# The Wf product of a two-layer graph network and routed FFN kernel, taken in rounded and rest parts in place of fp32

## The reference, cut to what matters

```python
def gnn(x, adj, W1, b1, W3, b3, Wf, bf):     # x: 2048 x 256, adj: 2048 x 2048, weights: 256 x 256
    h = relu(adj @ (x @ W1) + b1)
    h = relu(adj @ (h @ W3) + b3)
    return tanh(h @ Wf + bf)

x = x + gnn(layernorm(x), adj, ...)
x = x + routed_ffn(layernorm(x))             # 8 experts, top 2, hidden 1024, out = (silu(x@W1[e]) * (x@W3[e])) @ W2[e]
```

## Time and profile before

| | |
|---|---|
| median of 3 runs | 667.63 us (667.21 to 668.91) |
| profiled execution, its own time | 671.28 us |
| its span | 669.2 us |
| TensorE busy | 612.0 us (91%) |
| VectorE busy | 341.6 us (51%) |
| ScalarE busy | 312.5 us (47%) |
| GpSimd busy | 147.5 us (22%) |

### The profile page before, as it was taken

One profiled execution on the slowest core, in us unless ns is written; L12 is line 12 of the kernel. 1 busy time (PEld: TensorE's weight loads), 2 busy tenths in 40 slices (PEclk: granted clock), 3 DMA queues, 4 the chain that ended last, 5 costly groups with the idle time before them and its releaser, 6 DMA issues.

```text
span 669.2 us, 11466 instructions
## 1 busy us (share of the span) xinstructions
PE 612.0 (91%) x3472; PEld 519.8 (78%) x3473; DVE 341.6 (51%) x752; ACT 312.5 (47%) x589; POOL 147.5 (22%) x143
## 2 busy tenths in 40 slices
PE   1999999999999988989888999999999999999970
PEld 1888888887867676768767898888888888888860
DVE  3786434465646676636644333337333636377620
ACT  1567565766455465446522223335333536356520
POOL 3000000000000505027444123322332233223222
PEclk9999999999999999999989999999999999999985
DMA  8995000020002673521163022117111715376312
GB/s 303 359 333 203 5 1 1 0 95 1 1 3 92 123 177 119 159 64 41 17 194 90 10 33 34 29 21 219 32 28 19 219 32 147 88 211 166 80 29 32
DMA packets 34739, 63.74 MB, mean 95 GB/s; under 512 B 4954, under 2 KB 27100, under 8 KB 32636
## 3 DMA queue, kind: packets, MB, share of 16 engines
q1 hardware_dynamic: 26044, 52.32, 23.9%
q0 software_dynamic: 8224, 10.53, 9.7%
q10 hardware_dynamic: 432, 0.39, 0.2%
HBM read 54.02 MB, written 10.26 MB: 96 GB/s over the span
## 4 chain that ended last, share of the span: by engine, by line
PE 81%; DVE 4%; issue 4%; ACT 4%; DMA 3%; POOL 1%; SPq 0%; POOLq 0%; ACTq 0%; DVEq 0%
PE bank L1551 40%; PE bank L1420 8%; PE bank L1422 8%; PE bank L1421 8%; PE bank L1396 4%; PE bank L1598 4%; PE bank L1447 3%; DMA adj_s<-in_adj 2%; PE bank L1433 2%; PE bank L1384 2%; PE bank L1544 1%; DVE ring L915 1%; PE bank L1471 1%; POOL slot_rows L479 1%; PE bank L1445 1%
## 5 line engine op out<-in xcount | busy, mean ns | idle before, releaser
L1551 PE MATMUL bank<-ew,xeT 128*128 128x512 f32 x840 | 202.2, 395 | 4.6 <-DVE ew L1246 2.6
L1551 PEld LDWEIGHTS bank<-ew,xeT 128*128 128x128 f32 x840 | 154.7, 188 | 36.3 <-issue 4.2
L915 DVE TENSOR_TENSOR ring<-adj_s,ring 128x512 fp32r<-128x512 f32 x128 | 87.6, 689 | 76.5 <-ACT adj_s L596 40.8
L1551 PE MATMUL bank<-ew,heT 128*128 128x256 f32 x840 | 112.0, 291 | 4.7 <-issue 2.4
L1420 PE MATMUL bank<-ring,Z 128*128 128x512 f32 x256 | 110.1, 430 | 6.3 <-DVE ring L915 4.7
L1551 PEld LDWEIGHTS bank<-ew,heT 128*128 128x128 f32 x840 | 105.5, 196 | 6.2 <-issue 6.1
L1422 PE MATMUL bank<-ring,Z 128*128 128x512 f32 x256 | 100.6, 393 | 0.0
L1421 PE MATMUL bank<-ring,Z 128*128 128x512 f32 x256 | 100.2, 391 | 0.0
L512 POOL DMA_INDIRECT out<-y_st,idx_st x29 | 45.5, 1569 | 191.0 <-ACT y_st L748 169.0
L479 POOL DMA_INDIRECT slot_rows<-val,route x32 | 35.9, 1122 | 224.1 <-issue 222.4
L754 ACT ACTIVATE sil<-bank 128x512 f32<-128x512 f32 x58 | 34.6, 596 | 86.3 <-PE bank L1551 86.3
(11 more groups left out here) (183 smaller groups left out, 620.4 us busy)
## 6 DMA issues: line engine op xcount, KB each, us to landing
w_raw<-in_L_ffn_W SPq DMA_DIRECT2D x24, 1024.0 KB
adj_s<-in_adj SPq DMA_DIRECT2D x16, 1024.0 KB, 6.7
x_in<-in_x SPq DMA_DIRECT2D x4, 512.0 KB, 5.3
x_res<-in_x SPq DMA_DIRECT2D x4, 512.0 KB, 3.6
out<-x SPq DMA_DIRECT2D x4, 512.0 KB, 3.9
ffn_in_rows<-x_res SPq DMA_DIRECT2D x4, 512.0 KB
xg<-ffn_in_rows,idx POOLq DMA_INDIRECT x39
Wg<-in_L_gnn_W SPq DMA_DIRECT2D x2, 256.0 KB, 3.8
```

The lines of the kernel that those rows point to most:

```text
L915: nc.vector.tensor_tensor(lo, src, hi, ALU.subtract).then_inc(s_lo, 1)
L1551: last = nc.tensor.matmul(out_ap, stat[:, sl, k, :], w_at(k, wl), start=(k == k0 and sl == wl == 0), stop=(k == k1 - 1 and sl == 1))
```

## The change

The Wf product is taken like the others, from hi and lo parts. `hidden2` now handles one half `f` of the features at a time and writes two results, the rounded `hTs[:, 0]` and the whole `hTf[:, 1]`, with one activation each; its two halves stand at steps 1 and 2 of the next band in place of both at step 1. `h2_lo` on VectorE takes the rest at step 3. Wf itself is split once into `Wfs`, on VectorE, at step 8 of band 0. Each tile of `wf_rows` has six fp32r matmuls in place of two fp32 ones. `wf_rows` stands at steps 4 and 5 (before 2 and 3), and what comes after it moves too: `tanh` to 5 and 6 (3 and 4), `residual` to 6 and 7 (4 to 6), `spread` to 7 (6), the roots to 8 and 9 (7 and 8), `normal` to 9 and 10 (8 and 9), `xn_T` and `gate` one step later each. `top2`, `chosen`, `places`, `expert_order` and the expert's weights keep their steps. `hTs` is there once, while `hT` was there for two bands in turn: `hidden2` waits for the tiles of the band before. The last four gathered tiles go to `xge_b`, in the space of `Z`, so their gathers wait for the last step; the wait for `s_up` ahead of all of them is gone. Of `first_up(0, 0)` only the second half waits for `hidden2` of the last band, and that only for its first half.

```diff
@@ -73,12 +73,12 @@
         bf_hi = at("bf_hi", [2, D], F32R, 178)
-        hT = at("hT", [P, 2, KD, CW], F32, 176)
         hTs = at("hTs", [P, 2, KD, CW], F32R, 176)
...
         W3s = at("W3s", [P, 2, KD, D], F32R, 196)
+        Wfs = at("Wfs", [P, 2, KD, D], F32R, 198)
         route = at("route", [P, KB // 2], F32, 196)
@@ -93,7 +93,8 @@
         xeT0 = at("xeT0", [P, 2, KD, P], F32R, 172)
-        xge = at("xge", [P, EARLY, D], F32, 174)
+        xge_a = at("xge_a", [P, 2, D], F32, 174)
+        xge_b = at("xge_b", [P, EARLY - 2, D], F32, 156)
@@ -228,6 +229,8 @@
         s_w3s = sem("s_W3_split")
+        s_wfs = sem("s_Wf_split")
+        s_h2lo = sem("s_hT_layer2_lo")
         s_z2p = sem("s_z2_psum")
@@ -327,6 +330,10 @@
+        def first_rows(t):
+
+            return xge_a[:, t, :] if t < 2 else xge_b[:, t - 2, :]
+
         def first_xe_p(t):
@@ -483,7 +490,7 @@
                 nc.gpsimd.indirect_dma_start(
-                    out=xge[:, t, :], out_offset=None, in_=table[:, :],
+                    out=first_rows(t), out_offset=None, in_=table[:, :],
                     in_offset=bass.IndirectOffsetOnAxis(ap=first_idx[:, t:t + 1], axis=0),
@@ -529,9 +536,10 @@
             pool.wait_ge(s_xn1st, 32)
-            pool.wait_ge(s_up, CT * (NC - 1))
             for t in range(1, EARLY):
                 pool.wait_ge(s_xge, 16 * t)
+                if t == 2:
+                    pool.wait_ge(s_mm, 2 * S1)
                 first_gather(t)
@@ -610,16 +618,15 @@
-            def hidden2(c):
+            def hidden2(c, f):
                 act.wait_ge(s_mm, S1 + NT * (c + 1))
-                if c >= 2:
-                    act.wait_ge(s_up, CT * (c - 1))
+                if c >= 1:
+                    act.wait_ge(s_up, CT * c)
                 else:
                     act.wait_ge(s_z2p, NT)
-                for f in range(KD):
-                    last = nc.scalar.activation(hT[:, c % 2, f, :], acc[c % 2][f][:, :], ACT.Relu,
-                                                bias=bT[:, 1, f:f + 1])
+                for out_f in (hTs[:, 0, f, :], hTf[:, 1, f, :]):
+                    last = nc.scalar.activation(out_f, acc[c % 2][f][:, :], ACT.Relu, bias=bT[:, 1, f:f + 1])
                 last.then_inc(s_h2, 1)
@@ -650,12 +657,12 @@
-                if k in (3, 4):
-                    tanh(c, k - 3)
-                if k == 7:
+                if k in (5, 6):
+                    tanh(c, k - 5)
+                if k == 8:
                     roots(NC + c + 1)
-                if k in (10, 11):
-                    xn_T(c, k - 10)
+                if k in (11, 12):
+                    xn_T(c, k - 11)
                 if k == NT:
@@ -697,8 +704,8 @@
                     hidden1(s // NT - 1, jb - 1)
-                if jb == 1 and s > S1 + NT:
-                    hidden2(c - 1)
+                if jb in (1, 2) and s > S1 + NT:
+                    hidden2(c - 1, jb - 1)
                 if layer == 0 and c == NC - 1 and 2 <= jb < NT - CT + 2:
@@ -779,7 +786,8 @@
-            hidden2(NC - 1)
+            for f in range(KD):
+                hidden2(NC - 1, f)
             gap_exp(2)
@@ -924,6 +932,12 @@
                                         ALU.subtract).then_inc(s_hlo, 1)
+
+            def h2_lo(c):
+
+                dve.wait_ge(s_h2, KD * (c + 1))
+                nc.vector.tensor_tensor(hTs[:, 1, :, :], hTf[:, 1, :, :], hTs[:, 0, :, :].bitcast(F32),
+                                        ALU.subtract).then_inc(s_h2lo, 1)
@@ -1082,15 +1096,14 @@
-                tiles = {4: (0, 1), 5: (2,), 6: (3,)}.get(k, ())
-                residual(c, tiles)
-                if k == 6:
+                residual(c, {6: (0, 1), 7: (2, 3)}.get(k, ()))
+                if k == 7:
                     marked()
                     spread()
-                if k == 8:
+                if k == 9:
                     roots(NC + c + 1)
-                if k in (8, 9):
-                    normal(c, (2 * k - 16, 2 * k - 15))
+                if k in (9, 10):
+                    normal(c, (2 * k - 18, 2 * k - 17))
                 if k == NT - 2:
@@ -1169,6 +1182,13 @@
                     z_lo(NT - CT + jb - 7)
+                if layer == 1 and c == 0 and jb == 8:
+                    dve.wait_ge(s_z2p, NT)
+                    settle(nc.vector.tensor_copy(Wfs[:, 0, :, :], Wg[:, 2, :, :]))
+                    nc.vector.tensor_tensor(Wfs[:, 1, :, :], Wg[:, 2, :, :], Wfs[:, 0, :, :].bitcast(F32),
+                                            ALU.subtract).then_inc(s_wfs, 1)
+                if layer == 1 and c >= 1 and jb == 3:
+                    h2_lo(c - 1)
                 if layer == 1 and c >= 2:
@@ -1280,6 +1300,7 @@
             nc.vector.tensor_copy(first_idx[:, 1:EARLY], first_info[:, 1:EARLY, 0]).then_inc(s_fidx, 1)
+            h2_lo(NC - 1)
             residual(3, (0, 1))
@@ -1409,7 +1430,7 @@
                     else:
-                        pe.wait_ge(s_h2, n - 1 - NC)
+                        pe.wait_ge(s_h2, KD * (n - 1 - NC))
                     if n >= NC + 2:
@@ -1438,14 +1459,16 @@
                 for i in (2 * pair, 2 * pair + 1):
-                    pe.wait_ge(s_h2, c + 1)
+                    pe.wait_ge(s_h2lo, c + 1)
                     if c == 0:
+                        pe.wait_ge(s_wfs, 1)
                         pe.wait_ge(s_z2, NT)
...
                     for f in range(KD):
-                        last = nc.tensor.matmul(token_out(c, i), hT[:, c % 2, f, i * P:(i + 1) * P], Wg[:, 2, f, :],
-                                                start=False, stop=(f == KD - 1))
+                        for hl, wl in ((0, 0), (0, 1), (1, 0)):
+                            last = nc.tensor.matmul(token_out(c, i), hTs[:, hl, f, i * P:(i + 1) * P], Wfs[:, wl, f, :],
+                                                    start=False, stop=(f == KD - 1 and hl == 1))
                     last.then_inc(s_up, 1)
@@ -1481,12 +1504,12 @@
-                if k in (2, 3):
-                    wf_rows(c, k - 2)
-                if k in (9, 10):
-                    xn_T(c, k - 9)
-                if k in (11, 12):
-                    gate(c, k - 11)
+                if k in (4, 5):
+                    wf_rows(c, k - 4)
+                if k in (10, 11):
+                    xn_T(c, k - 10)
+                if k in (12, 13):
+                    gate(c, k - 12)
                 if k == NT:
@@ -1498,7 +1521,7 @@
                 for k in range(KD):
-                    last = nc.tensor.transpose(first_xe_p(t)[:, k * P:(k + 1) * P], xge[:, t, k * P:(k + 1) * P],
+                    last = nc.tensor.transpose(first_xe_p(t)[:, k * P:(k + 1) * P], first_rows(t)[:, k * P:(k + 1) * P],
                                                ident[:, :])
@@ -1552,9 +1575,11 @@
-            def up_half(h, buf, stat):
+            def up_half(h, buf, stat, after_last_block=False):
                 for m in range(2):
+                    if after_last_block and m == 1:
+                        pe.wait_ge(s_h2, KD * (NC - 1) + 1)
                     o = buf * EWS + m * H + h * HW
@@ -1605,11 +1630,9 @@
                     pe.wait_ge(s_xelo, t + 1)
-                if t == 0 and h == 0:
-                    pe.wait_ge(s_h2, NC)
                 if t >= 1:
                     pe.wait_ge(s_he, 2 * t - 1 + h)
-                up_half(h, rank, first_xeT(t) if t < EARLY else xeT)
+                up_half(h, rank, first_xeT(t) if t < EARLY else xeT, t == 0 and h == 0)
```

## The result

The changed kernel takes 676.25 us (median of five executions, 675.4 to 679.61) where the kernel before takes 668.74 beside it (667.21 to 668.91): ratio 1.012, 95% interval 1.010 to 1.014. It is slower, as predicted, by 7.5 us where 4.1 were forecast, and outside the range (675.0). The forecast started from 667.63, which is 1.1 us under what the kernel before takes here.

A forecast was written before the change was run, and what follows sets the result against it. TensorE at full clock was taken as the bound, its waits for lo parts decided by the ring. Layer 2 +5.4 us and the stretch behind -1.3 gave +4.1 on 667.63, so 671.7 us, range 667.5 to 675.

The forecast's parts named there:

- no term below is a clock term: TensorE has its full granted clock until near the end of the span, so every cost was worked out at full clock.
- the sum of the waits: Whole kernel: band 0 +0.2, band 1 +1.7, band 2 +3.3, band 3 +0.2, after layer 2 -1.3; sum +4.1 us.
- The Wf tile: Six fp32r matmuls take 1.22 us between tiles, 1.03 before a step, against 1.37 and 1.3; saves 0.86 a band.
- `expert_order`: Band 2, step 3: 2.2 us of VectorE loses its cover of Wf tiles; TensorE waits about 2.5 us ahead of step 4.
- `hidden2` and `h2_lo`: Bands 1 to 3, steps 1 to 4: waits of 0.3 us ahead of steps 3 and 4, about 0.6 a band.
- `gate` and `top2`: Steps 14 to the next band's 0: gate one step later delays `top2`; +1.2 us band 1, +1.4 band 2, +0.5 band 3.
- `residual` and `spread`: Steps 7 and 8: both share one step, so TensorE waits about 1.0 us at step 8; +0.5 a band, +1.0 in band 3.
- the weight half: Band 3, step 5: the waits of 1.0 us that the kernel before had at this weight half go away.
- After layer 2: Up product to first transposes: Wf tiles start earlier and run shorter, 1.05 us, and a 0.28 wait goes; -1.3 us.
- absorbed: Rival: slack at steps 3, 4, 8, 14, 15 is some 0.6 us larger, only `expert_order` costs; 665.7 us, chance 0.08.
- The gathers: Rival: behind layer 2, gathered rows rather than TensorE set the FFN's start, another 1.5 us; 673.3 us, chance 0.17.
- The skill's rule: Wf product: TensorE's rate halves for two-pass fp32, making the change 3.8 us dearer; the prediction went by the profile instead.

The follow-up runs named there:

- e9: Changed kernel with 9, 4 and 8 unread matmuls filling TensorE's waits ahead of band 2 steps 4 and 13 and band 3 step 8: 675.65 us, ratio 1.006.
- e4: Changed kernel's order of steps, but the Wf product in fp32 as before, without `h2_lo` and `Wfs`: 675.47 us, ratio 1.007 to the kernel before.
- e1: Changed kernel with `expert_order` moved from step 3 to step 5 of band 2: 672.95 us, ratio 1.002 to the kernel before.
- e3: Changed kernel with `top2` and `chosen` one step later in bands 0, 1 and 2: 676.7 us, ratio 1.007 to the kernel before.
- e6: Kernel before, with only the second half of the first up product waiting for the last band's `hidden2`: 666.86 us, ratio 0.997.
- c1: Changed kernel run again, unaltered, beside the kernel before: 676.2 us, ratio 1.012.
- e5: Changed kernel with Wf tiles back at steps 3 and 4 and what hangs on them one step earlier: 669.62 us, ratio 0.999 to the kernel before.
- e11: Kernel before, with unread transposes filling TensorE's wait for the slot lists (those meant for the last down product never ran): 670.04 us, ratio 0.997.

## Why the prediction failed in its range and held in its parts

**The step that failed** is the sentence of the first paragraph, "so no term below is a clock term". The page's row of granted clocks was read as a property of the kernel; it is one of what TensorE did in that execution. The change adds waits of 2.3, 1.1 and 2.0 us where band 2 had one of 1.5 and band 3 two of 0.9, and behind each of the three the clock can fall to half. By the three traces of the changed kernel that costs 4.9, 1.8 and 1.4 us in layer 2. With the 5.1 of the waits themselves that makes 6.5 to 10.0; measured were 7.5, 7.5 and 5.6, the last of them under it (both kernels also have drops behind layer 2, which come and go: from the first FFN tile to the end the three traces take 358.1, 356.7 and 360.3 us). The kernel with filled waits is 4.2 us over the kernel before in both of its comparisons. Between filled and bare waits the medians differ by 1.4 us on one chip, and by 3.3 if the comparisons on other chips are held together; how much of the 7.5 is the clock's stays open between these.

Of the 4.5 us between the forecast of 671.7 and the 676.25 measured, 1.1 is the start from 667.63 in place of 668.74, 1.0 is the sum of the waits (below), and the other 2.4 is what is left for the clock. Without the clock's share the kernel would have lain at 673 to 674 us, inside the range.

The clue was in the trace of before: two windows at 346 and 348 us show 0.57 and 0.58 behind a wait of 1.65 us, two at 646 and 648 show 0.66 and 0.50 behind one of 2.32. The row of the page averages the first into a single 8, and the text took the last two slices for the end of the program.

**The sum of the waits** was 4.1 and is 5.1 (e9). By its terms:
- The Wf tile: 1.21 us measured for 1.22 between tiles, but 1.13 for 1.03 where a step follows. The saving of 0.86 a band was over-sized: 0.47 (e4), less 0.24 for `h2_lo` at the step ahead.
- `expert_order`: 2.43 (e1) for 2.5. The wait stands where it was put and its cause is right.
- Band 0: +0.3 for +0.2; band 1 +1.9 for +1.7; band 2 +3.6 for +3.3; band 3 +0.4 for +0.2. That each is near its forecast is in part luck: the saving of the Wf tiles was over-sized by 0.6 a band, and other terms were too large or left out.
- `hidden2` and `h2_lo`: of the two waits of 0.3 a band, the one ahead of step 3 shows in band 1 only (step 2 takes 1.67 us there, 1.36 and 1.38 in bands 2 and 3). The sum of band 2 had left its 0.6 out.
- `gate` and `top2`: 1.45 (e3) for 1.2, but as a term that can't be had back: moved, it returns as a wait at the next band's first steps.
- `residual` and `spread`: step 8 of band 1 waits 0.89 us for about 1.0. Step 8 of band 3 goes from 0.89 to 2.02, +1.1 for +1.0, but that this makes a wait of 2.0 us, with a drop behind it in two traces of seven, is said nowhere. The wait of 0.89 at the weight half, ahead of step 6 of band 3, is gone, as it was to be.
- After layer 2: -1.1 for -1.3, since the wait of 0.28 stayed. e6 shows that -1.4 is to be had without the change.

**The rivals.** The waits weren't absorbed: steps 4, 8, 14 and 15 show theirs. The gathers didn't come either: in c1 and e9 the first FFN tiles stand later by what layer 2 is later, less 1.1. The range left out a cost that hangs on the waits, and every one of its cases was worked out at full clock.

**The skill's rule.** The Trainium skill, "Perfetto Trace Analysis", section "Engine Utilization", halves TensorE's rate for the form that it calls FP32_LOW_HIGH. Taken as the rate of a whole fp32 product, as the prediction took it, that would have made the new product dearer by 3.8 us. e4 shows the opposite sign: 0.47 us a band cheaper, and 1.13 against 0.98 us for a tile's matmuls. Taken as the rate of one of a product's two passes it agrees (0.25 against 0.12 us). The Trainium skill doesn't say there which is meant; the measurement decides.

## What to carry to other kernels

Moving work of TensorE to a later step takes the cover from whatever stood beside it in the other queues; look for the longest item there (here `expert_order`, 2.2 us) before the arithmetic is costed. A wait of TensorE of a microsecond or more is to be priced with its length and with a stretch at half clock behind it (1.4 to 1.8 us here), and judged on several traces, since one execution has the drop and the next has not. And a wait ahead of a product of which only the second half needs the data is worth moving (e6).

## What the runs showed of the hardware

In the 16 traces (the kernel before, the changed one and the 14 runs), from 150 us on, every stretch at half clock but the one at the very end of the program begins in the last 0.6 us of a wait of TensorE or within 1.8 us behind it. Of 28 waits of 2.2 us and more 23 were followed by one, of 53 between 1.5 and 2.2 us 5, of 87 between 0.85 and 1.5 us 5, all five of these at waits of 1.08 to 1.15 us. Place counts as well as length: 24 of the 28 stand at two places behind layer 2 (the slot lists, 7 of 8 with a drop, and the last down product, 13 of 16), and the wait of 1.1 us at (2, 13) had a drop in 4 of 7 traces, the one of 2.0 at (3, 8) in 2 of 7, that of 1.7 at (2, 15) in none of 5. The same wait of the same kernel fell on either side: 2.31 and 2.32 us with a drop, 2.33 without. A drop costs 1.4 to 1.8 us in the layer's steps, where the same step can be read with and without one. The Trainium skill, "TensorE: Matmul & The Clock Gate", section "Part 1: The HAM clock gate", says that a gate sets the array's clock to full or half by how busy TensorE has been; the windows agree: 0.50 or 1.00, and means between them only where a drop begins or ends. No run here shows why one execution draws a drop and the next doesn't, or why a shorter wait at one place has it more often than a longer one at another.

It also explains part of the kernel's own spread. Of 23 executions of the kernel before beside e1, those with a mean clock of 0.988 took 667.6 to 668.6 us, those of 0.983 and 0.984 669.9 to 670.7, those of 0.980 and 0.981 671.8 to 673.1. The levels are less clean elsewhere: beside c1 executions at 0.986 took 668.1 to 671.2 us, beside e11 those at 0.985 took 667.5 to 670.4. e5's profiled execution had no drop but the one at the program's end: clock 0.988, 667.01 us.
